# Attention outputs with V as the stationary operand in two column tiles, row sums from the exponential

## What is computed

```python
q, k, v = (to_heads(q), to_heads(k), to_heads(v))
sim = jnp.einsum('bid,bjd->bij', q, k) * scale
sim = sim + _cope(q, sim, pos_emb)     # cumulative sums of sigmoid(sim) from the right, a table of 64
attn = jax.nn.softmax(sim, axis=-1)
out = jnp.einsum('bij,bjd->bid', attn, v)
out = out.reshape(B, h, N, d).transpose(0, 2, 1, 3).reshape(B, N, h * d)
return out @ Wout + b_out
```

## Time and profile before

| | |
|---|---|
| time, median of 3 runs | 2726.79 us (2726.04 to 2726.97) |
| span of the profiled execution | 2722.5 us |
| self-attention | to about 2248 us |
| DVE busy from 1000 to 1500 us | 483.7 us |
| PE busy from 1000 to 1500 us | 475.8 us |
| ACT busy from 1000 to 1500 us | 296.9 us |

### The profile page before, as it was taken

The page is one execution under the profiler, slowest core; times in us unless marked ns, Lnnn a source line. Parts: engine busy times, 40 slices in busy tenths (PEclk is TensorE's granted clock), DMA queues, the critical chain, the costliest instruction groups (busy, mean ns, idle before and its releaser), DMA issues. The chain is left out here.

```text
span 2722.5 us, 69322 instructions
## 1 busy us (share of the span) xinstructions
PE 2562.4 (94%) x18175; PEld 2259.5 (83%) x18175; DVE 2256.0 (83%) x5821; ACT 1501.2 (55%) x2487; POOL 214.1 (8%) x283
## 2 busy tenths in 40 slices
PE   6999999999999999999999999999999997999997
PEld 5888888888888888888888888888888885777776
DVE  6999999999999999999999999999999980222222
ACT  4655565556556555565555655555555552344442
POOL 0000000000000000000000000000000000111111
PEclk9999999999999999999999999999999998999998
DMA  2111111111111111111111111111110102001100
GB/s 81 35 39 35 39 35 39 35 39 35 37 35 37 33 37 33 39 35 39 35 39 35 39 35 39 35 36 37 34 28 25 45 10 74 26 31 35 35 23 8
DMA packets 126696, 97.59 MB, mean 36 GB/s; under 512 B 24078, under 2 KB 124559, under 8 KB 126672
## 3 DMA queue, kind: packets, MB, share of 16 engines
q1 hardware_dynamic: 126672, 97.29, 12.5%
HBM read 13.21 MB, written 2.10 MB: 6 GB/s over the span
## 5 line engine op out<-in xcount | busy, mean ns | idle before, releaser
L494 PE MATMUL out<-V,probsT 128*128 (+1 forms) x8192 | 959.5, 273 | 0.0
L494 PEld LDWEIGHTS out<-V,probsT 128*128 128x128 f32 x8192 | 944.5, 192 | 0.9
L361 ACT ACTIVATE probsT<-ring 128x512 f32<-128x512 f32 x1024 | 584.5, 597 | 503.4 <-PE ring L482 503.4
L482 PEld LDWEIGHTS ring<-ident,probs 128*128 128x128 f32 x4096 | 474.7, 141 | 250.3 <-issue 170.9
L482 PE MATMUL ring<-ident,probs 128*128 128x128 f32 x4096 | 580.1, 274 | 98.4 <-DVE k_lo L704 98.2
L369 ACT ACTIVATE probs<-Sc,nbias 128x1024 f32<-128x1024 f32 x512 | 543.2, 1112 | 232.7 <-DVE nbias L674 232.5
L657 DVE TENSOR_REDUCE mx<-Sc 128x1 f32<-128x1024 f32 (+1 forms) x640 | 636.3, 994 | 0.9 <-PE Sc L474 0.8
L474 PE MATMUL Sc<-k_hi,q_now 128*128 (+1 forms) x1024 | 469.5, 458 | 17.2 <-ACT probs L369 10.3
L621 DVE COPY_PREDICATED z<-mask,z 128x96 f32<-128x96 int16 (+6 forms) x896 | 422.1, 471 | 30.8
L474 PE MATMUL Sc<-k_lo,q_now 128*128 (+1 forms) x1024 | 406.6, 397 | 0.0
L297 POOL TENSOR_TENSOR prod<-frac,z 128x350 f32<-128x350 f32 x128 | 142.5, 1113 | 2085.2 <-DVE z L644 2085.2
(11 more groups left out here) (117 smaller groups left out, 2392.5 us busy)
## 6 DMA issues: line engine op xcount, KB each, us to landing
q_far<-q SPq DMA_DIRECT2D x128, 128.0 KB, 2.0
q_now<-q SPq DMA_DIRECT2D x128, 128.0 KB, 2.0
xv<-xT SPq DMA_DIRECT2D x113, 128.0 KB, 2.2
k_hi<-k_hi SPq DMA_DIRECT2D x128, 64.0 KB, 1.9
k_lo<-k_lo SPq DMA_DIRECT2D x128, 64.0 KB, 1.9
at<-attn SPq DMA_DIRECT2D x16, 512.0 KB, 3.2
q<-stage SPq DMA_DIRECT2D x120, 64.0 KB, 1.9
probs<-in_x_dram SPq DMA_DIRECT2D x4, 512.0 KB, 5.5
```

Of the source, the lines that this page charges most:

```text
L361: nc.scalar.activation(probsT[:, u, 4 * s:4 * s + 4, :], ring[(k + s) % 2][:, :].rearrange("p (t q) -> p t q", q=P), ACT.Copy).then_inc(sl ...
L482: last = nc.tensor.transpose(ring[(k + s) % 2][:, j * P:(j + 1) * P], probs[:, u, (4 * s + j) * P:(4 * s + j + 1) * P], ident[:, :])
L494: last = nc.tensor.matmul(out[:, 0:VW], probsT[:, u, t, :], V[:, h % 4, t, :], start=t == 0, stop=t == NT - 1)
```

## The change

In `outputs` V becomes the stationary operand (64 columns) and the transposed probabilities stream. Even key tiles accumulate on partitions 0 to 63 of `out`, odd ones on 64 to 127. The result is transposed and in two halves: ACT copies it to `halves` (`empty_halves`), and one product with `fold`, two unit matrices above each other, adds the halves and turns them (`turn`) into columns 128 to 191 of `out`. The row sums come from the exponentials' `accum_out`, two halves that DVE adds (`add_halves`). The current head's V is loaded to its own tile `V_now` once a head. Three tiles share memory with others. On DVE inversions and scalings move.

```diff
+        V_now = sb("V_now", [P, NT, C])
+        halves = sb("halves", [P, 2, P])
+        fold = sb("fold", [P, C])
...
-        flo = sb("flo", [P, 2, W])
-        frac = sb("frac", [P, 2, W])
+        flo = rnd
+        frac = cut
...
-        corr = sb("corr", [P, 2, W])
+        corr = prod
...
+            def load_values(g):
+                sp.dma_start(V_now[:, :, :], V[:, (g // PAIRS) % 4, :, :]).then_inc(v_in, 16)
...
             def body(g, late=False, proj=True, tile=True, far=True, now=True, head=False):
                 base = slots_before(g, late)
+                if head:
+                    wait_apart(sp, out_full, g * 2, waited)
+                    load_values(g)
                 if far:
...
+            def empty_halves(g, u):
+                act.wait_ge(out_full, g * 2 + u + 1)
+                nc.scalar.activation(halves[:, u, :], out[:, 0:P], ACT.Copy).then_inc(halves_out, 1)
+
             def exps(g, u):
...
-                    nc.scalar.activation(probs[:, u, cols], Sc[:, cols], ACT.Exp,
-                                         bias=nbias[:, u:u + 1]).then_inc(exp_done, 1)
+                    nc.scalar.activation(probs[:, u, cols], Sc[:, cols], ACT.Exp, bias=nbias[:, u:u + 1],
+                                         accum_out=sums[:, u, half:half + 1]).then_inc(exp_done, 1)
...
                 if not first:
 
+                    empty_halves(g - 1, 0)
                     transposed(1, base, 0)
...
                 exps(g, 0)
+                if not first:
+                    empty_halves(g - 1, 1)
                 if val:
-                    if not first:
-                        act.wait_ge(out_full, g * 2)
                     values(g, base, k)
...
                 if wait_read and tiles[0] == 0:
                     pe.wait_ge(out_read, g * 2 + u)
+                if tiles[0] == 0:
+                    wait_apart(pe, v_in, g // PAIRS * 16 + 16, waited)
                 for t in tiles:
                     if t % 4 == 0:
                         pe.wait_ge(slot_out, base + k + t // 4 + 1)
-                    last = nc.tensor.matmul(out[:, 0:VW], probsT[:, u, t, :], V[:, h % 4, t, :],
-                                            start=t == 0, stop=t == NT - 1)
+                    half = t % 2 * C
+                    last = nc.tensor.matmul(out[half:half + C, 0:P], V_now[:, t, :], probsT[:, u, t, :],
+                                            start=t < 2, stop=t >= NT - 2)
...
+            def turn(g, u):
+                pe.wait_ge(halves_out, g * 2 + u + 1)
+                nc.tensor.matmul(out[:, TURN:TURN + C], halves[:, u, :], fold[:, :],
+                                 start=True, stop=True).then_inc(turned, 1)
...
                     if n < 2:
                         logits(g, 0, n + 2)
+                    if n == 1 and not first:
+                        turn(g - 1, 0)
...
                     if n < 2:
                         logits(g, 1, n + 2)
+                    if n == 1 and not first:
+                        turn(g - 1, 1)
...
+            def add_halves(g, u):
+                dve.wait_ge(exp_done, g * 4 + u * 2 + 2)
+                nc.vector.tensor_tensor(rowsum[:, u:u + 1], sums[:, u, 0:1], sums[:, u, 1:2],
+                                        ALU.add).then_inc(summed, 1)
...
                 if chain:
                     scan_floors(c)
+                if not first:
+                    scale(g - 1, 0)
                 window_max(g, 0, 1, 2, 4)
...
-                if not first:
-                    invert(g - 1, 1)
                 bank_max(g, 1, 0, 0, 1, 2)
                 if not first:
-                    scale(g - 1, 1)
+                    add_halves(g - 1, 1)
                 if chain:
                     shift(c, 4)
                 add_window(g, 1)
+                if not first:
+                    invert(g - 1, 1)
                 if chain:
                     shift(c, 3)
+                if not first:
+                    scale(g - 1, 1)
                 window_max(g, 1, 1, 3, 3)
...
-                invert(g, 0)
+                add_halves(g, 0)
                 if scan:
                     scan_positions(c + 1)
-                scale(g, 0)
+                invert(g, 0)
                 if scan:
                     round_positions(c + 1)
```

More of the change, by code:

```diff
@@ L253, in _, with body @@
             weights(1)
-            def body(g, late=False, proj=True, tile=True, far=True, now=True):
+            def load_values(g):
+                sp.dma_start(V_now[:, :, :], V[:, (g // PAIRS) % 4, :, :]).then_inc(v_in, 16)
+            sp.wait_ge(slot_out, 8 + 2 * PAIRS)
+            load_values(0)
+            def body(g, late=False, proj=True, tile=True, far=True, now=True, head=False):
                 base = slots_before(g, late)
+                if head:
+                    wait_apart(sp, out_full, g * 2, waited)
+                    load_values(g)
                 if far:
@@ L270, in body @@
                     load_now(g + 1)
-            with sp.Fori(0, LASTV // PAIRS - 1) as h:
-                with sp.Fori(0, PAIRS) as t:
+            with sp.Fori(0, PAIRS) as g:
+                body(g)
+            weights(2)
+            with sp.Fori(1, LASTV // PAIRS - 1) as h:
+                body(h * PAIRS, head=True)
+                with sp.Fori(1, PAIRS) as t:
                     body(h * PAIRS + t)
                 weights(h + 2)
-            with sp.Fori(LASTV - PAIRS, LASTV) as g:
+            body(LASTV - PAIRS, head=True)
+            with sp.Fori(LASTV - PAIRS + 1, LASTV) as g:
                 body(g)
             weights(H - 1, values=False)
-            with sp.Fori(LASTV, LASTP) as g:
+            body(LASTV, tile=False, head=True)
+            with sp.Fori(LASTV + 1, LASTP) as g:
                 body(g, tile=False)
@@ L283, in _ @@
             load_early(sp, A, A["ctx_in"])
-            with sp.Fori(LASTP, G - 2) as g:
+            body(LASTP, late=True, proj=False, tile=False, head=True)
+            with sp.Fori(LASTP + 1, G - 2) as g:
                 body(g, late=True, proj=False, tile=False)
@@ L289, in _ @@
         def _(pool):
[L290 removed]
+            nc.gpsimd.memset(fold[:, :], 0.0).then_inc(consts, 1)
             pool.wait_ge(consts, 1)
@@ L293, in _ @@
                            channel_multiplier=0).then_inc(consts, 1)
+            for half in range(2):
+                pool.wait_ge(consts, 2 + half)
+                nc.gpsimd.affine_select(out=fold[:, :], in_=fold[:, :], compare_op=ALU.not_equal, fill=1.0,
+                                        base=-half * C, pattern=[[-1, C]], channel_multiplier=1).then_inc(consts, 1)
             def body(c):
@@ L677, in invert @@
             def invert(g, u):
-                dve.wait_ge(out_full, g * 2 + u + 1)
-                nc.vector.reciprocal(rsum[:, u:u + 1], out[:, C:VW]).then_inc(rsum_done, 1)
+                wait_apart(dve, summed, g * 2 + u + 1, waited)
+                nc.vector.reciprocal(rsum[:, u:u + 1], rowsum[:, u:u + 1]).then_inc(rsum_done, 1)
+            def add_halves(g, u):
+                dve.wait_ge(exp_done, g * 4 + u * 2 + 2)
+                nc.vector.tensor_tensor(rowsum[:, u:u + 1], sums[:, u, 0:1], sums[:, u, 1:2],
+                                        ALU.add).then_inc(summed, 1)
             def scale(g, u):
@@ L683, in scale @@
                 dve.wait_ge(rsum_done, g * 2 + u + 1)
-                nc.vector.tensor_scalar(attn[:, t * 2 + u, bass.ds(h * C, C)], out[:, 0:C], rsum[:, u:u + 1],
-                                        None, ALU.mult).then_inc(out_read, 1)
+                wait_apart(dve, turned, g * 2 + u + 1, waited)
+                nc.vector.tensor_scalar(attn[:, t * 2 + u, bass.ds(h * C, C)], out[:, TURN:TURN + C],
+                                        rsum[:, u:u + 1], None, ALU.mult).then_inc(out_read, 1)
             def q_rest(s, par):
@@ L794, in _ @@
             body(G - 1, chain=False, scan=False, proj=False)
+            scale(G - 1, 0)
+            add_halves(G - 1, 1)
             invert(G - 1, 1)
```

15 lines of the change are left out of this document (13 added, 2 removed).

## The result

The changed kernel takes 2911.7 us (median of 4 runs, 2905.2 to 2918.1) against 2726.9: a ratio of 1.068, 95% interval 1.066 to 1.070. The profiled execution, the longest of the four, has a span of 2916.3 us, 193.8 more than before. The forecast was +74, so the sign was right and the size was not.

What follows compares the result with a forecast made beforehand. DVE's instruction chain was taken as the bound, 17.24 us a pair. Its own +0.18 and a late chain's +0.45 over 112 pairs gave 70.6 us; with the other pairs and the tail +74.4, forecast 2801 us, range 2746 to 2912.

Steps and rivals of the forecast that it cites:

- What bounds the kernel: Attention stage: DVE's own chain of instructions sets the period, 17.24 us a pair; PE's product with V lies beside it.
- The moved scaling: DVE's scaling of (g-1,0), now behind scan_floors, holds PE some 2.4 us; the resulting chain reaches DVE 0.45 us late.
- the hand-over to PE: From DVE's scaling to PE's product: 0.28 us plus 0.1 for the V_now wait, so PE resumes at 2.89.
- from projection to q: From the projection's start on PE to ACT's q copy: 1.46 us, so the copy starts at 4.89.
- the row sums: ACT's exponentials with a sum: 0.1 us extra each, bounds 0 and 0.28.
- the passes at 0.055: PE's product with V: even and odd key tiles overlap, 0.055 us a pass, freeing 3.5 us of PE a pair.
- Hand-over from the fold to DVE: From the fold's end on PE to DVE's scale(g-1,1): 0.05 us, so the scaling starts at 10.81.
- DVE's own part: DVE's moved scalings and reciprocals plus two new one-column adds: 0.62 us removed, 0.80 put back, +0.18 a pair.
- Rival 4: PE's stall in each pair lowers its clock to 1.2 GHz, doubling 3.1 us from product to logits: above 3000 us; chance 0.05.
- Rival 2: The product's column tiles on PE don't overlap, passes 0.11 us apart: about 2902 us; chance 0.22.
- Rival 3: Not slower: one-column instructions on DVE cost almost nothing, falling in its idle time: 2704 to 2727 us; chance 0.08.
- Rival 1: The chain from PE back to DVE just fits, leaving only DVE's own +0.18 a pair: 2750 us; chance 0.13.

Runs made afterwards that it cites:

- The last experiment: The changed kernel with row sums, inversions and scalings taken off DVE, now given the old product instead of the column tiles: 2689.4 us, 0.986.
- the filled stall: The changed kernel with nine unit-matrix products added on PE, taking up about 2 us of its wait for the scaling: 2858.0 us, 1.049.

## Why the prediction was wrong

**What bounds the kernel** was right: DVE's chain, with the product beside it. The last experiment shows it, as both products give the same period.

**The moved scaling** was right in mechanism and place. The move is enough for a full-clock pair as long as the changed kernel's, as the kernel before with this one move shows. It isn't all of the loss: with the scaling first, or back in its old place, 95 and 100 us are left. The table above has every step from the scaling to the fold within 0.12 us of the forecast: the hand-over to PE (2.77 against 2.89), 1.51 from projection to q against 1.46, the row sums' 0.09 an exponential against 0.1, the passes at 0.055. The sum was wrong at both of its ends, and it left out a step.

- *Hand-over from the fold to DVE*, put at 0.05. The fold takes 0.33, and the kernel with the rests moved shows the scaling's start 0.34 behind its end: 11.03, not 10.81, so 0.22 a pair too little.
- *The step that is missing.* The prediction follows k_hi to the exponentials at 5.72 and never to DVE's q rest, which waits for it too. Side by side the two look harmless, k_hi done at 5.66 and q's rest due some 0.2 later. But from k_hi's end to q's rest 0.70 us pass, and the next instruction starts 0.53 after its start, where before it was 0.34. q's rest is late by 0.5 and what stands behind it by 0.2 more, which puts the scaling at 11.12, another 0.09 too little in the sum, and hides the fold's lateness: DVE's waits for the fold, which the prediction wanted as its proof, are not among the 19 rows that the view of waits gives for the 500 us.
- *DVE's own part*, +0.18. The two scalings (0.18 and 0.20 from start to start) and the one-column instructions (0.06 to 0.07 each, where they don't stand between scan and rounding) cost no more than forecast. What failed is the 0.22 credited for scale(g,0) removed from between scan and rounding. From the scan's start to the rounding's were 1.77 us with it (1009.08 to 1010.85) and are 1.79 without (1004.88 to 1006.67), and in both the rounding starts 0.15 behind the scan's end: it stood in a gap in which the rounding waits for the scan anyway. From window_max(g,1) to the next pair's start the prediction takes 0.13 off; it was 6.99 before and is 7.02: 0.16 too little.

Together 0.63 + 0.22 + 0.09 + 0.16 = 1.10 for a full-clock pair, against 1.08 in the pair shown. Without the fall of the clock the kernel takes 2858 us, as the filled stall shows, against the 2801 forecast. So what failed are the hand-over from the fold to DVE (0.05, measured 0.34), the wait of q's rest for k_hi, which the chain lacks, the credit of 0.22 for the removed scaling, of which nothing came, and the clock, which was left out of the sum and costs about as much as these three together.

**Rival 4, the clock,** had 0.05 and came true in about half of the pairs, for 54 to 59 us. The prediction weighed mean busy shares of two stretches of 10 us from the start of the kernel and asked for the mean of the pair; what decided was one stall: with it filled, the clock stayed up. In the pair shown the clock fell 1.1 us after PE had resumed; over all pairs it fell between 0.3 us before and 1.6 behind. The price was wrong as well: not all of the 3.1 us from product to logits adds to DVE's path. In most slowed pairs it is the projection up to q's rest, 0.96 on average; where only the rest of the product is slow, it reaches DVE by the logits and adds 0.46.

**Rival 2** is refuted by the passes at 0.055. The sentence of the Trainium skill (TensorE: Matmul & The Clock Gate, The mechanism) on which it rests, that weight loads overlap running matmuls only where row groups differ, does not hold here: all passes use all rows. That tiles on different columns work in parallel (the Trainium skill, TensorEngine Tiling (Array Packing), Key Properties) agrees with the trace, as far as passes on different tiles stand near each other in the queue.

**Rival 3** is refuted too: the added one-column instructions cost about what the reciprocal does. **Rival 1** had the hand-over to PE right (0.28, with nothing on top for the V_now wait), but the row sums aren't free and both late ends of the chain reach DVE.

The range, 2746 to 2912, held the time at its very edge, and that is luck: it reached there for rival 2, which did not come true.

Two points stay open. Why about every other stall brings the clock down and not each, with 2.18 and 2.19 us ahead of them, isn't shown by any run; from 804 to 1066 us pairs with a full and with a slowed projection alternate strictly. And how the 0.70 us from k_hi to q's rest divide is only partly known: the order of the waits is 0.2 of it; the rest (semaphore, the address of q2's column, the start of the instruction) was not taken apart.

## What to carry to other kernels

When a step moves on the bound engine, follow every reader of what then comes late, back to each instruction of that engine that waits for it, and price each hand-over between engines by a row of the same kind (0.28 to 0.70 us here), not by the distance between instructions of one engine. An instruction that stands where its neighbour waits was free here, and removing it brought nothing; look at the gap between what stands on either side of it. Put back there with one more wait ahead of it, it cost 0.22. And a stall of PE may have to be charged twice, as time and as clock, even when its mean load stays high: here it was 54 us.

## What the runs showed of the hardware

- Two float32 products on 64 columns each overlap fully (0.055 us a pass against 0.109) if they alternate in PE's queue, and as well where four passes of one stand ahead of four of the other, but hardly when sixteen do (0.098 on average).
- An exponential with a sum leaves an instruction of its own on ACT, `ACTIVATION_READ_ACCUMULATOR`, 0.19 us long, of which 0.09 shows up in the distance to the next.
- A stall of 2.2 us per pair of 18 lowered the clock to 1.2 GHz in 61 of 118 pairs ahead of the projection's end and in about ten behind it. Where stalls of 1.16 and 0.80 us stand close together (the scaling back in its old place) it fell in a third of the pairs, where they are 1.00 and 0.80 (the scaling first) in ten. In the changed kernel it fell between 0.3 us before PE was at work again and 1.6 after, and stayed low for some 3 us; in the kernel before with the scaling moved it stayed low for 10 us in 19 pairs.
- A short DVE instruction can cost more than its duration: the scaling is 0.18 to 0.22 us from start to start between other work, and 0.53 at the head of the pair, where 0.33 pass ahead of it in which the profile shows no wait.
